# An inverse square root on VectorE instead of a square root on ScalarE, and two gate products ahead of each group of down products

## The reference

```python
def _ln_fused_l2_bwd(x, target, gamma, beta):
    D = x.shape[-1]
    mu = x.mean(-1, keepdims=True)
    std = jnp.sqrt(x.var(-1, keepdims=True) + EPS)          # EPS = 1e-6
    xh = (x - mu) / std
    gxh = (gamma * xh + beta - target) * gamma
    return (D * gxh - gxh.sum(-1, keepdims=True) - xh * (gxh * xh).sum(-1, keepdims=True)) / (D * std)

def step(carry, x):
    W1_s, b1_s = carry
    xq, xk, xv, eta_mb = x
    Z1 = xk @ W1_s + b1_s
    grad = _ln_fused_l2_bwd(Z1, xv - xk, ln_w, ln_b)
    ...
    W1_new = W1_s - (last_eta * xk).swapaxes(-1, -2) @ grad
    b1_new = b1_s - jnp.sum(last_eta * grad, axis=-2, keepdims=True)
```

```python
g = jnp.einsum('th,ih->ti', xf, gate_w) * gate_s
u = jnp.einsum('th,ih->ti', xf, up_w) * up_s
hdn = jax.nn.silu(g) * u
out = jnp.einsum('ti,hi->th', hdn, down_w) * down_s
```

## Time and profile before

| | |
|---|---|
| median of 3 runs | 2395.42 us (2394.92 to 2399.89) |
| profiled execution | 2388.66 us, its span 2386.8 us |
| PE busy | 2040.8 us, 86% |
| VectorE busy | 1416.5 us, 59% |
| ScalarE busy | 1051.1 us, 44% |
| GpSimd busy | 662.5 us, 28% |
| PE, VectorE, ScalarE busy in 240 to 840 us | 523.1, 389.1, 329.7 us of 600 |

### The profile page before, as it was taken

One profiled execution on the slowest core, in us unless ns is written; L12 is line 12 of the kernel. 1 busy time (PEld: TensorE's weight loads), 2 busy tenths in 40 slices (PEclk: granted clock), 3 DMA queues, 4 the chain that ended last, 5 costly groups with the idle time before them and its releaser, 6 DMA issues. The chain is left out here.

```text
span 2386.8 us, 32172 instructions
## 1 busy us (share of the span) xinstructions
PE 2040.8 (86%) x11528; PEld 1434.4 (60%) x11528; DVE 1416.5 (59%) x2599; ACT 1051.1 (44%) x2151; POOL 662.5 (28%) x554
## 2 busy tenths in 40 slices
PE   4886888989888896697996895899999999999998
PEld 2664766656565564243442453677777777777776
DVE  3552555667676734526111425788888878788885
ACT  3221555555555553302000313655555555555553
POOL 4343555455454443000000003222222222222220
PEclk9898998999999998898998997999999999999999
DMA  6575646335335331411224844023232113222201
GB/s 208 209 247 159 232 138 238 108 113 185 93 122 171 108 119 35 158 36 71 75 84 147 309 155 195 36 73 128 83 115 106 71 71 115 109 89 85 106 36 54
DMA packets 131117, 297.93 MB, mean 125 GB/s; under 512 B 19088, under 2 KB 65680, under 8 KB 124304
## 3 DMA queue, kind: packets, MB, share of 16 engines
q1 hardware_dynamic: 130960, 295.88, 35.8%
HBM read 221.66 MB, written 74.19 MB: 124 GB/s over the span
## 5 line engine op out<-in xcount | busy, mean ns | idle before, releaser
L1748 ACT ACTIVATE probs<-bank,nmax 128x512 f32<-128x512 f32 x256 | 176.6, 690 | 366.3 <-DVE nmax L1817 366.3
L1844 DVE TENSOR_TENSOR p_lo<-bank,p_hi 128x512 fp32r<-128x512 f32 x256 | 177.1, 692 | 163.2 <-ACT p_hi L1768 163.2
L1619 POOL TENSOR_TENSOR qk_lo<-roped,qk_hi 32x512 fp32r<-32x512 f32 x128 | 165.0, 1289 | 193.8 <-ACT qk_hi L1742 121.2
L1817 DVE TENSOR_REDUCE nmax<-bank 128x1 f32<-128x512 f32 x256 | 175.1, 684 | 9.6 <-PE bank L62 8.2
L1609 POOL TENSOR_TENSOR roped<-rot 128x512 f32<-128x512 f32 x32 | 41.2, 1289 | 458.5 <-DVE rot L1791 458.4
L1674 PE MATMUL bank<-id,probs 128*128 128x128 f32 x1024 | 155.6, 274 | 10.4 <-DVE probs L1824 10.4
L1824 DVE TENSOR_SCALAR probs<-probs,rsum 128x512 f32<-128x512 f32 x256 | 157.5, 615 | 9.1
L1131 DVE SCALAR_TENSOR_TENSOR pt<-bank,t_mask 128x256 f32<-128x256 f32 x256 | 91.9, 415 | 117.2 <-PE bank L923 115.8
L60 PE MATMUL bank<-xs,ffn_w 128*128 128x512 f32 x352 | 152.7, 434 | 9.9 <-issue 8.2
L1674 PEld LDWEIGHTS bank<-id,probs 128*128 128x128 f32 x1024 | 126.3, 140 | 51.1 <-DVE probs L1824 20.4
L1768 ACT ACTIVATE p_hi<-bank 128x512 fp32r<-128x512 f32 x256 | 151.2, 591 | 10.6 <-PE bank L1674 8.7
(11 more groups left out here) (256 smaller groups left out, 5018.3 us busy)
## 6 DMA issues: line engine op xcount, KB each, us to landing
ffn_w<-ffn_pieces SPq DMA_DIRECT2D x120, 512.0 KB, 3.7
uvo<-uvo_pieces SPq DMA_DIRECT2D x16, 2048.0 KB, 7.9
wq<-wq_pieces SPq DMA_DIRECT2D x16, 1536.0 KB, 6.8
ffn_pieces<-stage SPq DMA_DIRECT2D x30, 512.0 KB, 4.4
xs<-xn_pieces SPq DMA_DIRECT2D x4, 2048.0 KB, 7.8
gup<-in_gup SPq DMA_DIRECT2D x4, 2048.0 KB, 9.6
wk<-wk_pieces SPq DMA_DIRECT2D x16, 512.0 KB, 3.5
ffn_w<-ffn_pieces SPq DMA_DIRECT2D x16, 384.0 KB, 3.5
```

The lines of the kernel that those rows point to most:

```text
L1619: nc.gpsimd.tensor_tensor(qk_lo[r, G % 2, kq, hh, :], roped[r, pair, :], qk_hi[r, G % 2, kq, hh, :].bitcast(F32), ALU.subtract).then_inc(r ...
L1748: nc.scalar.activation(probs[:, u % 3, :], banks[u % 3][:], ACT.Exp, bias=nmax[:, u % 4:u % 4 + 1], scale=1.0, accum_out=rsum[:, u % 4:u % ...
L1817: nc.vector.tensor_reduce(nmax[:, u % 4:u % 4 + 1], banks[u % 3][:], axis=X_AXIS, op=ALU.max, negate=True).then_inc(max_done, 1)
L1844: nc.vector.tensor_tensor(p_lo[:, H % 2, :, q], banks[3 + u % 2][:].rearrange("p (k q) -> p k q", k=NBLK), p_hi[:, H % 2, :, q].bitcast(F3 ...
```

## The change

1. In the scan step, ScalarE's warm, its square root st_s and the semaphores var_done and std_done go, and VectorE's reciprocal too. Instead VectorE forms 1/sqrt(v/16 + eps) itself: one tensor_scalar for the variance, one tensor_scalar on the bits of the number taken as an integer (an estimate of the inverse root), and three Newton rounds of three instructions. All eleven are links of the chain.
2. In ffn_order, two gates of the next third stand in front of a third's downs instead of one, and the block starts with two gates; later gates move up accordingly.

```diff
@@ ffn_order @@
-            order = [("gate", 0, 0)]
+            order = [("gate", 0, 0), ("gate", 0, 1)]
             for a, (lo, hi) in enumerate(THIRDS):
                 for i in range(lo, hi):
-                    order += [("gate", a, i)] if i > lo else []
+                    order += [("gate", a, i)] if i > lo + 1 else []
                     order += [("up", a, i)]
-                order += [("gate", a + 1, hi)] if a + 1 < len(THIRDS) else []
+                order += [("gate", a + 1, hi), ("gate", a + 1, hi + 1)] if a + 1 < len(THIRDS) else []
                 order += [("down", a, o) for o in range(NF)]
@@ ScalarE @@
-                            nc.scalar.activation(warm[:], eps[:, 0:1], ACT.Sqrt)
                             act.wait_ge(z_ready, n + 1)
                             nc.scalar.activation(sqz[:], zbank[:, 0:HX], ACT.Square).then_inc(sq_done, 1)
-                            act.wait_ge(var_done, n + 1)
-                            nc.scalar.activation(st_s[:], st_v[:], ACT.Sqrt, bias=eps[:, 1:2], scale=1.0 / HD).then_inc(std_done, 1)
@@ VectorE @@
+                    def rsqrt(y, v, a, b):
+                        ch.link(nc.vector.tensor_scalar(v[:], v[:], 1.0 / HD, TTT_EPS, op0=ALU.mult, op1=ALU.add))
+                        ch.link(nc.vector.tensor_scalar(y[:].bitcast(I32), v[:].bitcast(I32), -0.5, float(0x5F3759DF), op0=ALU.mult, op1=ALU.add))
+                        for _ in range(3):
+                            ch.link(nc.vector.tensor_tensor(a[:], y[:], y[:], ALU.mult))
+                            ch.link(nc.vector.scalar_tensor_tensor(out=b[:], in0=v[:], scalar=-0.5, in1=a[:], op0=ALU.mult, op1=ALU.mult))
+                            ch.link(nc.vector.scalar_tensor_tensor(out=y[:], in0=b[:], scalar=1.5, in1=y[:], op0=ALU.add, op1=ALU.mult))
...
-                            nc.vector.reduce_sum(st_v[:], hd(sqz[:]), axis=X_AXIS).then_inc(var_done, 1)
-                            dve.wait_ge(std_done, n + 1)
-                            ch.link(nc.vector.reciprocal(st_r[:], st_s[:]))
+                            ch.link(nc.vector.reduce_sum(st_v[:], hd(sqz[:]), axis=X_AXIS))
+                            rsqrt(st_r, st_v, st_s, st_p)
```

More of the change, by code:

```diff
@@ L7 @@
 F32R = mybir.dt.float32r
+I32 = mybir.dt.int32
 ALU = mybir.AluOpType
@@ L631, in build @@
             st3 = s("st_3", [P, 3, NX])
-            warm = s("warm", [P, 1])
+            st_p = s("st_p", [P, NX])
             st_a, st_b, st_x = st3[:, 0, :], st3[:, 1, :], st3[:, 2, :]
@@ L641, in build @@
             delta = zbank[:, HX:2 * HX]
-            names = ("w_done z_ready sq_done var_done std_done sg_done sgbd_dve sgbd_act ssum_done d_done wx_dve wx_act snap_done sz_done wsx_done "
+            names = ("w_done z_ready sq_done sg_done sgbd_dve sgbd_act ssum_done d_done wx_dve wx_act snap_done sz_done wsx_done "
                      "kz_done kt_ready kt_done qbd_done gbd_done p_ready pt_done o_done base_done ocopy_done osq_done ovar_ready ostd_done orec_done "
@@ L645, in build @@
                      "grad_in xs_in acc_in acc_out")
-            (w_done, z_ready, sq_done, var_done, std_done, sg_done, sgbd_dve, sgbd_act, ssum_done, d_done, wx_dve, wx_act, snap_done, sz_done, wsx_done,
+            (w_done, z_ready, sq_done, sg_done, sgbd_dve, sgbd_act, ssum_done, d_done, wx_dve, wx_act, snap_done, sz_done, wsx_done,
              kz_done, kt_ready, kt_done, qbd_done, gbd_done, p_ready, pt_done, o_done, base_done, ocopy_done, osq_done, ovar_ready, ostd_done, orec_done,
```

## The result

The changed kernel takes 2444.9 us (median of 4 runs, 2441.9 to 2447.9) against 2395.2 for the kernel before: the ratio of the two is 1.0227, 95% interval [1.0207, 1.0247], and by the medians alone it is 1.0208. It is 2.1 to 2.3% slower. The forecast was 2432 in a range of 2409 to 2461, so sign and range hold, and the middle is 13 us too low. The profiled execution took 2444.7 us (span 2442.9), 56.0 more than the profiled one of before.

A forecast was written before the change was run, and what follows sets the result against it. The prediction took VectorE's chain, last at state_update in 29 of 32 scan steps, to bound the kernel. Its terms, 50 + 7 - 21 - 4 + 5 = +37 us, put on the median 2395.42, gave 2432 us, range 2409 to 2461.

The forecast's parts named there:

- What bounds the kernel: In the scan, VectorE's chain arrives last at state_update in 29 of 32 steps, so added chain time lengthens the step.
- The links: Between reduction and xh, eleven VectorE links replace 0.66 us, adding 1.73 us a step in 29 steps: +50 us.
- Collisions: In the scan's chain, GpSimd holds up the new small VectorE instructions, 0.25 us a step: +7 us, 0 to +19.
- ScalarE's relief: In the scan, 19 table loads instead of 50 and no warm make late Squares earlier: -21 us, -13 to -30.
- Rival 1: ScalarE bounds more than the Squares; all its saving, 56 us, comes through, giving 2385 us, slightly faster; chance 0.08.
- rival 2: A tie: relief of 40 us and no added collisions, +6 us or less, some 2398 us; chance 0.08.
- rival 3: Links collide with GpSimd in half or more steps and the clock falls: +69 us or more, 2465; chance 0.12.
- rival 4: Silu and square-root loads still alternate through o_std, ScalarE gains nothing: +62 us; no separate chance given.
- The gates: In the FFN order, two gates before the downs remove step 4's hole behind state_update: -4 us, 0 to -6.
- PE's clock: Behind state_update, more idle time lowers the granted clock in three or four more stretches: +5 us, 0 to +12.
- All stages behind the scan as before: Behind the scan, all stages were to stay as before; no term in the sum.

The follow-up runs named there:

- e4_psum: The changed kernel with the reduction's output and the iterate held in PSUM, still eleven links; 2419.9 us.
- e2_gates_only: The kernel before with only the new order of jobs (two gates in front of the downs); 2390.5 us.
- e13_busy_sized: The changed kernel with 108 useless products in front of the wait for state_update, in 18 steps alone; 2427.1 us.
- e10_busy_after: The changed kernel with 256 useless products in front of the wait for state_update; 2471.0 us.
- e8_share_gates: The kernel before with the two gates and one feed-forward trip moved in front of state_update in steps 9 to 31; 2393.7 us.
- e12_busy_all: The changed kernel with statistics in PSUM, two Newton rounds, one feed-forward trip moved in front of state_update in steps 9 to 31, and 130 useless products; 2435.8 us.

## Why the prediction was right, and where it was off

1. **What bounds the kernel**: right. The chain is last in 30 steps, and nearly each microsecond of it counts: three links fewer, 27 us of chain, gave 24 us of time, some of it through the clock behind state_update.
2. **The links, +50**: right. 2.34 us in a step free of collisions against 0.66, times 32, is +54 on the chain, and 4.1 us of the chain's growth were covered by PE's list, which the prediction had put as 29 steps of 32. Step 20, on time in both kernels, grew by 1.71 us from z_product to state_update, where 1.73 was worked out.
3. **Collisions, +7 (0 to 19)**: as a net figure inside its bounds, but by another account. The new stretch holds 28.5 us of them (103.4 less 32 times 2.34), and 16.9 us went from the stretch behind xh, so the net is +11.6. That most of them would only move was right. That nine of the eleven links are exposed was not: all eleven are. What the term didn't see is that they are avoidable: e4_psum is 25 us faster with the same eleven links.
4. **ScalarE's relief, -21**: the lateness fell by 25.3 us, 24.6 of it in the eleven steps that were named. The differences listed for these steps add up to 20.9 and not to 22, so the term has nothing left in it for what was said not to come through in steps 6 and 7. Taking the relief away again costs 12 us in the changed kernel. Rival 1, the relief as large as the loads' own length, would have left the kernel at 2385 us; it is out, as are rival 2 (2398) and rival 3 (2465), and rival 4 by the 19 loads. And no drain was seen: each of the 50 loads before took 1283 ns and started within 19 ns of the end of the instruction in front, and behind 48 of them the next one started within 12 ns. By the 2.66 us a switch of the Trainium skill ("ScalarE: Activation LUTs", section "What ACT_TABLE_LOAD costs") the prediction had put the relief at some 40 us; 25.3 came, so here the trace does not agree with that figure.
5. **The gates, -4 (0 to -6)**: the mechanism was right to the place. Step 4's stretch fell by 4.0 us and step 6's hole is there still, 4.81 us. The size was not: over all runs they give nothing, and a gain of 4 us lies outside the interval. They also move ScalarE's and GpSimd's work in other steps (in e2_gates_only steps 3, 9 and 25 are longer by 1.8 to 3.1 us, 6 and 8 shorter by 3.4 and 4.0), which the term left out.
6. **PE's clock, +5 (0 to 12)**: this is the term that was mis-sized. The stretches behind state_update grew by 13.3 us although step 4's lost 4.0, so by 17. I had counted three or four more slow stretches of 1.5 us; fourteen grew, by 0.9 to 1.9 us, since idle time per step rose from 2.0 to 3.2 us in the mean and steps with 2 to 4 us of it can pay as well (step 1: 2.28 us idle, 5.92 for 4.36). Not each does: step 5, with 2.64 us idle, kept 4.34 us and the full clock. What tells the two apart is open. e13_busy_sized got 13 us of it back in the profile.
7. **All stages behind the scan as before**: wrong by 10.9 us in the profiled execution, though the cause lies in the execution that I started from (below). Against it stand the 4.0 us by which step 0 came earlier, so 6.9 us were left outside the steps. Placing the sum on the median, 6.8 us above that execution, covered just that, which was luck.

The sum z_product to state_update, 50 + 7 - 21 = +36, came out at +35.9. The agreement to a tenth is luck: the parts were 54 for the links, 11.6 for the collisions, -25.3 for the relief and -4.1 covered by PE. What was missing in the forecast is the clock, 12 us.

## What to carry to other kernels

Before work is moved from an idle engine to the one that carries the chain, count dependent instructions: here eleven links of 0.21 us replaced two hops, a square root and a reciprocal that took 0.66 us, and the relief of ScalarE, 12 us where it was taken away again, did not pay for them. Where VectorE's small links run beside GpSimd, give each an operand in PSUM; that alone was worth 25 us. And an idle time of PE can be paid twice, once for itself and once in the granted clock of what follows: price it from stretches of the same work behind long and short waits before calling it free.

## What the runs showed of the hardware

**Useless work can make a kernel faster.** The scan of e13_busy_sized is 14.7 us shorter (0.72 against 1.00 of the granted clock, above), with more work on PE. It wants idle time that is surely there: 256 such products, in eleven steps behind a wait for an eviction, cost 26 us (e10_busy_after against after).

**The clock fell in one of two identical stretches.** The 10.9 us behind the scan: `w_rot` times `w_uqt`, 96 matmuls of 128x64, each with a weight load, in the preparation of the attention, before and after (group, busy us, mean ns, idle before):

```profile
L1424 PE MATMUL bank<-w_rot,w_uqt 128*128 128x64 f32 x96 | 11.4, 276 | 0.4 <-DVE piece_lo L1491 0.2
```

```profile
L1431 PE MATMUL bank<-w_rot,w_uqt 128*128 128x64 f32 x96 | 20.7, 422 | 0.0
```

The granted clock of those stretches, with the columns as above:

```profile
1349.00:1361.00 12.00, 11.62 (x128) 11.20 (x128) 6.08 (x20) 5.00 (x15) 0.00 (x0) 1.00 0.97 359
```

```profile
1398.00:1419.50 21.50, 21.50 (x132) 21.47 (x132) 9.48 (x29) 7.71 (x24) 0.00 (x0) 0.51 0.87 322
```

PE was hardly idle in either (11.62 of 12 us busy, and all of 21.5), and the code is the same; at 0.51 it ran at the 1.2 GHz level for all of the stretch, and 9.3 us are lost; the other 1.6 us behind the scan were not traced to a cause. Of the fourteen profiled kernels of this case only the kernel before and e8_share_gates were at the full clock all through it (e12_busy_all and e13_busy_sized for a part, 18.5 us), so it goes with neither the change nor the length of the scan. The runs of one kernel fit with this: e13_busy_sized took 2417.5 and 2417.6 us in two runs and 2426 to 2432 in four, 9 to 14 us more. The mean granted clock of the whole execution was 0.953 and 0.956 in the two and 0.949 to 0.951 in the four. That the two had the full clock in this stretch is argued from that, not shown, and what decides it is open. Whoever compares two profiles should look for such a stretch first: here it made 9 of 56 us of difference that no edit had caused.
